# Convolution and neighbourhood attention on one core: the softmax division and the output projection moved to the last tiles of a chunk, the queries' third parts and two row fills moved earlier

## What is computed

```python
x = x + _L0_conv_ref(_gn(x), L0_conv_W)            # grouped 3x3 convolution
x = x + _L1_conv_ref(_gn(x), ...)                  # the following, per image:
    q, k, v = qkv[0] * SCALE, qkv[1], qkv[2]       # (x @ w_qkv + b_qkv), 16 heads
    logits[i] = einsum('bnhwd,bnhwd->bnhw', q, k at (start_h + a, start_w + b)) + rpb bias
    attn = softmax(logits over the 49 positions of the window)
    out = sum_i attn[i] * (v at the same position)
    return out @ w_proj + b_proj
```

## Time and profile before

| | |
|---|---|
| median of 3 runs | 1418.45 us (1417.29 to 1420.87) |
| profiled execution | 1416.97 us, its span 1415.2 us |
| mean granted TensorE clock | 0.849 |
| busy | PE 82%, DVE 63%, ACT 48%, POOL 41% |

### The profile page before, as it was taken

How to read it: one execution, slowest core, us unless ns; L and a number is a source line. 1 busy time by engine, 2 the same in 40 slices (tenths; PEclk the granted TensorE clock), 3 DMA queues, 4 the chain that set the end, 5 groups by cost and what they waited for, 6 DMA issues and landing times.

```text
span 1415.2 us, 38266 instructions
## 1 busy us (share of the span) xinstructions
PE 1158.0 (82%) x12441; PEld 788.0 (56%) x12441; DVE 896.2 (63%) x2136; ACT 673.7 (48%) x1867; POOL 579.8 (41%) x1278
## 2 busy tenths in 40 slices
PE   3799999455989788878979897988888888969893
PEld 3455555353656465555656664655556555646561
DVE  2422222696868577667757685867577677858682
ACT  2100000602665566555646565666556565646662
POOL 3000000500637265444545472736365454626371
PEclk8799999655999898878878897988798889989996
DMA  9200000242565466737473655556475737464662
GB/s 254 54 33 32 32 33 34 81 106 41 123 125 147 94 158 132 159 85 164 107 149 98 141 133 107 144 101 166 76 175 125 162 84 161 110 131 116 125 149 60
DMA packets 142490, 159.51 MB, mean 113 GB/s; under 512 B 29952, under 2 KB 119888, under 8 KB 142040
## 3 DMA queue, kind: packets, MB, share of 16 engines
q1 hardware_dynamic: 141432, 153.13, 47.0%
q0 software_dynamic: 864, 3.90, 0.9%
HBM read 86.09 MB, written 70.47 MB: 111 GB/s over the span
## 4 chain that ended last, share of the span: by engine, by line
PE 55%; DMA 18%; DVE 13%; issue 8%; SPq 4%; POOL 1%; ACT 1%; DVEq 0%; POOLq 0%; ACTq 0%
PE PS L1088 14%; PE PS L1194 10%; PE PS L1157 9%; DMA area<-mcol 8%; DMA sums<-packed 7%; PE PS L1178 5%; PE PS L1100 5%; PE PS L1204 4%; PE PS L1171 4%; DVE bias L941 3%; DVE area L983 3%; PE PS L1141 3%; DVE S L1004 2%; SPq L488 2%; DMA area<-x 2%
## 5 line engine op out<-in xcount | busy, mean ns | idle before, releaser
L578 POOL TENSOR_TENSOR halves<-masked 128x96 f32<-128x96 f32 (+1 forms) x512 | 202.7, 396 | 493.4 <-DVE masked L1015 492.9
L1157 PE MATMUL PS<-area 97*128 97x48 bf16 (+1 forms) x4112 | 257.8, 211 | 67.4 <-issue 37.3
L1004 DVE TENSOR_TENSOR S<-PS,bias 128x384 f32<-128x384 f32 (+1 forms) x513 | 283.4, 553 | 43.6 <-PE PS L1157 27.5
L761 ACT ACTIVATE S<-S 128x384 f32<-128x384 f32 (+1 forms) x512 | 269.1, 536 | 81.8 <-DVE S L1004 43.2
L1194 PE MATMUL PS<-S,VT 128*36 128x96 f32 (+1 forms) x4096 | 299.9, 273 | 9.9 <-ACT S L761 9.9
L754 ACT ACTIVATE VT<-PS 128x128 f32<-128x128 f32 x449 | 125.6, 280 | 359.2 <-PE PS L1141 356.1
L1157 PEld LDWEIGHTS PS<-area 97*128 97x128 bf16 x4112 | 186.6, 105 | 160.2 <-issue 91.0
L1194 PEld LDWEIGHTS PS<-S,VT 128*36 128x36 f32 x4096 | 180.9, 121 | 160.7 <-issue 92.0
L1015 DVE TENSOR_TENSOR masked<-PS,cst 128x192 f32<-128x192 f32 (+1 forms) x512 | 181.5, 355 | 102.3 <-PE PS L1194 95.9
L994 DVE TENSOR_REDUCE mcol<-PS 128x6 bf16<-128x480 f32 (+2 forms) x297 | 181.3, 611 | 98.7 <-PE PS L1178 98.7
L1088 PE MATMUL PS<-area 128*128 128x392 f32 x576 | 191.6, 495 | 3.9 <-DVE area L883 3.9
(11 more groups left out here) (87 smaller groups left out, 1141.7 us busy)
## 6 DMA issues: line engine op xcount, KB each, us to landing
k_parts<-area SPq DMA_DIRECT2D x204, 168.0 KB, 3.0
area<-k_parts SPq DMA_DIRECT2D x33, 1008.0 KB, 7.8
q_parts<-area SPq DMA_DIRECT2D x204, 98.0 KB, 2.2
area<-q_parts SPq DMA_DIRECT2D x66, 294.0 KB, 7.6
xa<-x_mid SPq DMA_DIRECT2D x18, 392.0 KB, 4.9
late<-x_mid SPq DMA_DIRECT2D x17, 392.0 KB, 6.9
out<-area SPq DMA_DIRECT2D x17, 392.0 KB, 5.9
den<-sums SPq DMA_DIRECT2D x66, 98.0 KB
```

The lines of the kernel that those rows point to most:

```text
L578: nc.gpsimd.tensor_tensor(h, m[:, :, 0:2, :], m[:, :, 2:4, :], ALU.add).then_inc(s["half"], 1)
L761: nc.scalar.activation(S[:, n % 4, 0:cols], S[:, n % 4, 0:cols], ACT.Exp).then_inc(s["probs"], 1)
L1004: nc.vector.tensor_tensor(S[:, n % 4, 0:cols], PS[:, SCORE + n % 2, 0:cols], bias[:, at:at + cols], ALU.add).then_inc(s["biased"], 1)
L1157: last = mm(PS[:, SCORE + n % 2, cols * g:cols * (g + 1)], key_rows[a][0:PEAK_ROW + 1, g, key:key + 128], query_rows[a][0:PEAK_ROW + 1, g, ...
```

## The change

Four tables or tests move work within a chunk, and SP's order in odd chunks is rewritten. Nothing is computed that was not computed before.

- `divide` from tile 12 to tile 14 (DVE).
- `project_out`: both halves at tile 15, before `weigh(14)`, in place of one at tile 13 and one at tile 14 (PE). `keep_projection` stays at tile 15 (ACT), since its test was `MISC_PROJECT + 2`.
- `keep_second` of the queries from tile 14 to tile 11 of the even chunk (ACT).
- `subtract_second` of the queries from tiles 1 and 2 of the odd chunk to tiles 14 and 15 of the even one (POOL).
- In odd chunks SP stores the queries' third parts before it collects the denominators, and issues `fill_queries` right behind `fill_keys`, ahead of `spread_reciprocals`.

```diff
-        MISC_PROJECT, MISC_TURN = 13, 24
+        MISC_PROJECT, MISC_TURN = 15, 24
...
-        FIRST_BANK, RECIPROCAL, NORMALIZE, NEXT_IMAGE, RESIDUAL = 1, 6, 12, 30, 20
+        FIRST_BANK, RECIPROCAL, NORMALIZE, NEXT_IMAGE, RESIDUAL = 1, 6, 14, 30, 20
...
-        SECOND = {8: ("k", 0), 10: ("k", 1), 14: ("q", 0)}
+        SECOND = {8: ("k", 0), 10: ("k", 1), 11: ("q", 0)}
...
-        THIRD = {10: ("k", 0), 11: ("k", 1), 12: ("k", 2), 13: ("k", 3), 17: ("q", 0), 18: ("q", 1)}
+        THIRD = {10: ("k", 0), 11: ("k", 1), 12: ("k", 2), 13: ("k", 3), 14: ("q", 0), 15: ("q", 1)}
...
                     if c % 2:
                         store_keys(j, i + 1, True)
+                        store_queries(j, i + 1, True)
                         collect_denominators(j, c)
-                        store_queries(j, i + 1, True)
                         fill_keys(j, c + 1)
+                        fill_queries(j, c + 1)
                         spread_reciprocals(j, c)
-                        fill_queries(j, c + 1)
                         move_maxima(j, c + 1, False)
...
-                        if n == MISC_PROJECT + 2:
+                        if n == MISC_PROJECT:
                             keep_projection(j, c)
...
-                        if MISC_PROJECT <= n < MISC_PROJECT + 2:
-                            project_out(j, c, n - MISC_PROJECT)
+                        if n == MISC_PROJECT:
+                            for g in range(2):
+                                project_out(j, c, g)
```

## The result

| | before | changed |
|---|---|---|
| median | 1417.87 us (4 runs) | 1432.15 us (1427.23 to 1432.97, 4 runs) |
| profiled execution, its span | 1416.97, 1415.2 us | 1432.97, 1431.2 us |
| mean granted clock | 0.849 | 0.845 |

The ratio is 1.0092, 95% interval 1.0062 to 1.0121. Forecast was 1415; the case "ScalarE's new wait decides" stood at 1434.

A forecast was written before the change was run, and what follows sets the result against it. PE's waits for `divide`, 86.1 us in all, were taken as the bound; +0.6 us per even and -0.8 per odd chunk, times 16, gave -3.2 us from 1416.97 (1413.8); adding the median's 1.5 us: 1415, range 1391 to 1440.

The forecast's parts named there:

- ScalarE's new wait decides: Even chunks, rival: PE's 2.3 us idle keeps clock at 0.50 through projection, +1.8 us per even chunk; 1434 us, chance 0.20.
- Steps 1 and 2: Even chunk before `weigh(12)`: ACT's query rounding waits for POOL, PE idles 2.3 us instead of 1.25; start 635.15.
- Step 4: Even chunk: `divide` at tile 14 behind three spread heads, ready at 638.4, PE there at 638.2; 0.2 us added.
- Step 5: Even chunk's sum: projection halves 1.7 us at full clock, next chunk at 640.25; +0.6 us taken from -0.1 to +1.8.
- Steps 6 to 9: Odd chunk: key fill 1.7 us sooner, query fill delays reciprocals by 3.0, landing 1.2 later; maxima 1.9 sooner.
- Steps 10 and 11: Odd chunk's end: another projection half paid, -0.45 us; clock returning sooner, 0.35 us gained; -0.8 us together.
- The signs that were to show the forecast right: `weigh` waits for ACT 2 us (even); L1157 for `mcol` 4, reciprocals 7, maxima 5.3 (odd); `divide` wait below 20.

The follow-up runs named there:

- Run 1: Changed kernel with the queries' second parts rounded at tile 12 instead of 11 on ACT: 1.0111 of the kernel before.
- run 3: Kernel before with only the division moved to tile 14 and both projection halves to tile 15; tables and SP order untouched: 1.0216 of the kernel before.
- Run 10: Run 1's kernel with the division ahead of the heads of the spread on DVE: 1.0053 of the kernel before.
- Run 6: Changed kernel, even chunks' division and projection at old tiles; odd chunks: reciprocals' write before query fill, maxima before reciprocals' read: 0.9607 of kernel before.
- runs 9 and 12: Run 6 with odd chunks' division and projection at old tiles: 0.9843; Run 6 with old tables and third-part store order: 0.9786; both of the kernel before.
- run 7: Kernel before with only the maxima and query fill issued ahead of the reciprocals' read in odd chunks: 0.9999 of the kernel before.
- run 4: Changed kernel with the query fill issued behind the reciprocals again: 1.0032 of the kernel before.

## Why the prediction was wrong

The forecast was -3.2 us for the profiled execution and the changed kernel's took +16.0, 14.9 of it in the loop.

- **Steps 1 and 2 held.** `weigh(12)` at 635.15 by the working, and measured; ACT waits 1.37 us for POOL, PE 2.23 us for ACT. That is 1.05 us of idle more by the working; over all even chunks it is 1.0 (2.66 us for 1.66).
- **Step 4 held.** Division ready at 638.4 by the working, 638.2 measured (643.14 + 1.05 - 5.98). Beside it the prediction reads "no pair with the division" of VectorE and POOL. There is one: POOL's L581 took 0.90 us at 633.22 (0.29 at 631.61) while the division of rows 5 ran 1.15 us, where one that POOL leaves alone takes 0.98; in the changed kernel POOL's third part took 1.55 us at 643.33 in place of 0.82. The division itself did not get slower by the change, so the sum does not hang on it.
- **Step 5 is the step that failed**: "The clock is 0.50 from 631.4 and back at 1.00 from 638.3, when the projection would begin, so I take a value nearer the lower end: +0.6 us". I took the end of a low stretch from one chunk. In the sixteen even chunks of the kernel before, it ends from 27.5 to 31.6 us after the chunk's start (29.6 in that one), and both halves took 2.8 to 2.9 us as a mean. With 1.7 us I had counted on a gain that was to pay for the longer idle. It did not come: 2.98 us in the chunk shown, 2.93 and 2.65 as means. Measured were +2.2 and +0.7 us, a mean of +1.4, the mean within the bounds of that step (-0.1 to +1.8), chunk 0 above them. 0.8 us times 16 is 13 us.
- That chunk 2 came out near the +0.6 us is in part luck: that value was picked between bounds, and its halves took 2.65 us where the lower end has 1.7. Why the low stretch of chunk 0 became 3 us longer (4.7 to 7.7 as a mean) and that of chunk 2 only 1.3 (5.5 to 6.8) stays open.
- **Steps 6 to 9 held.** Over all odd chunks of the changed kernel the reciprocals landed 19.0 us after the chunk's start (18.7 by the working) and the maxima 25.5 us (25.4), against 17.6 and 27.3 before. The 3.0 us taken for the query fill was right to some tenths. By the ring order of the Trainium skill (DMA: Bandwidth & Descriptors, Queues, rings and completion order) the trace agrees once more: with both fills in front the small write took 7.6 us.
- **Steps 10 and 11** gave -0.8 us as a mean: measured -1.0 in chunk 1 and 0.0 in chunk 3, so -0.5. In chunk 3 PE's waits in the tile steps grew from 4.5 to 5.3 us, where the reciprocals landed up to 20.7 us after the start, and the idle at the loop's end from 5.3 to 6.1. The prediction put the second at nothing. It lies between 3.8 and 9.8 us in single turns of the runs here, and none of them tells what sets it. 0.3 us times 16 is 5 us.

13 and 5 us make up the distance from -3.2 to +15 in the loop.

The signs that were to show the forecast right all came: no wait for the division, PE held 2.2 to 2.7 us by ACT, a wait of 4.3 us for the maxima and 7.6 us for the reciprocals in the chunk shown; and the mean granted clock moved by 0.004. None of them looked at what the projection takes, which was the step in doubt.

The rival that came nearest is the first, at 1434 us. It had +1.8 us per even and -0.8 per odd chunk, where +1.4 and -0.5 were measured. Its mechanism is half of what the runs show: the projection stays at half clock, but it had been there before, and the loss is the idle itself. Its name was too narrow. Run 1 took ACT's hold away and the even chunks kept most of their loss; run 3 has a good part of the loss without any hold. Run 10 took both waits away and the even chunks were back, with the projection still at half clock. I had both waits in steps 2 and 4, added 0.2 us for the second, and did not say that each alone would keep the projection late.

What I had not put as a rival at all is the place of the maxima in SP's order. PE's wait for `divide` was counted as what the change aims at, but in odd chunks both chains go through one queue, in which the maxima, ready early, stand behind a wait for the reciprocals. Run 6 shows that this was the largest loss left in the changed kernel: with it mended, the late projection in odd chunks and the early second and third parts gain 2.4% and 1.8% (runs 9 and 12).

## What to carry to other kernels

When a wait is moved later so that its data may land, look at what the engine met behind it before: work that stood between two waits was free, and is paid once it stands behind both. Then look for the second chain on the same DMA queue; a small transfer whose data is ready belongs ahead of a wait on that queue. Here it gave nothing by itself, in the kernel before (run 7), and 0.961 of that kernel's time together with the late projection in odd chunks and the early second and third parts (run 6), where the changed kernel stands at 1.009. Price TensorE work by what it takes over all turns of the loop, and not by where the clock rose in one of them.

## What the runs showed of the hardware

- In every even chunk of the kernel before the granted clock stood at 0.50 for 3.4 or 6.8 us, beside or just behind idles of PE of 0.29, 0.62 and 1.25 to 1.86 us, and in the changed kernel for 6.8 or 10.2 us with idles of 0.29, 0.62 and 2.23 or 2.72 us. The two stretches of 10.2 us had the shorter of these idles, 2.23 us, so the idle's length alone does not set that of the stretch. Two halves of the projection took 2.98 us at half clock and 1.58 us at full clock.
- The same kernel, run 4's, gave times from 1410 to 1432 us on one chip, and the kernel before only 1410 to 1419. I did not find out why; its profile was taken at 1420.
- 24.5 KB written to HBM took 1.5 us alone, 5.9 us behind a fill of 1008 KB issued 1.4 us earlier, and 7.6 us behind that and another 588 KB, issued 3.4 and 2.5 us earlier.
